# Row chains of a four-layer graph network laid further apart, and eight row scalings moved from GpSimd to ScalarE

## What is computed

```
layer 0: XW = mobius_matvec(W, x); gamma = 2 / max(1 - |XW|^2, eps)
         two_mean = (adj @ (gamma * XW)) / clamp(adj @ (gamma - 1))
         result = expmap0(relu(logmap0(mobius_scalar_mul(rowsum(adj), mobius_scalar_mul(0.5, two_mean)))))
layer 1: a_hat = adj + I; d = rowsum(a_hat)^-0.5; result = (d * a_hat * d @ x) @ W.T + b
layer 2: dis = clip(rowsum(adj), 1)^-0.5; sim = cosine similarities of all rows of x (4096 x 4096)
         attn = softmax(beta * sim * adj, axis=1)
         result = (dis * adj * dis) @ x - x + sigmoid(alpha) * (attn @ x - x)
layer 3: msg = relu((adj @ x) @ W_msg.T + b_msg); result = gru_cell(msg, x, W_ih, W_hh, b_ih, b_hh)
```

## Time and profile before

| | us |
|---|---|
| median of 3 runs | 1555.27 |
| lowest and highest | 1553.88, 1557.45 |
| profiled execution, its own time | 1554.37 |
| its span, first to last instruction | 1552.6 |
| PE busy | 1340.4 (86%) |
| PE weight loads busy | 1026.7 (66%) |
| DVE busy | 1063.1 (68%) |
| ACT busy | 1068.0 (69%) |
| POOL busy | 627.2 (40%) |
| DMA | 413 MB, mean 266 GB/s |

### The profile page before, as it was taken

The page is one execution under the profiler, slowest core; times in us unless marked ns, Lnnn a source line. Parts: engine busy times, 40 slices in busy tenths (PEclk is TensorE's granted clock), DMA queues, the critical chain, the costliest instruction groups (busy, mean ns, idle before and its releaser), DMA issues. The chain is left out here.

```text
span 1552.6 us, 21041 instructions
## 1 busy us (share of the span) xinstructions
PE 1340.4 (86%) x7640; PEld 1026.7 (66%) x7640; DVE 1063.1 (68%) x1928; ACT 1068.0 (69%) x1368; POOL 627.2 (40%) x457
## 2 busy tenths in 40 slices
PE   4599998999887989896499999999998889998885
PEld 4599898898774777772265656656666666665553
DVE  5245555555656989986477887887877986766664
ACT  4578877788675766754386877878778566565563
POOL 4302212222344342336976776767666720000000
PEclk8699999999998999998799999999999999998998
DMA  9399999999955978881386867878776868666640
GB/s 311 124 364 347 342 349 333 341 343 358 314 206 198 336 255 320 304 348 70 147 309 221 321 247 272 275 248 303 256 279 207 296 251 364 213 237 228 224 169 14
DMA packets 114808, 413.08 MB, mean 266 GB/s; under 512 B 10000, under 2 KB 23568, under 8 KB 90128
## 3 DMA queue, kind: packets, MB, share of 16 engines
q1 hardware_dynamic: 106256, 407.54, 73.2%
q10 hardware_dynamic: 8448, 4.20, 0.9%
HBM read 340.40 MB, written 71.30 MB: 265 GB/s over the span
## 5 line engine op out<-in xcount | busy, mean ns | idle before, releaser
L1330 DVE TENSOR_TENSOR part_l<-arena,part_h 128x1024 fp32r<-128x1024 f32 x256 | 326.4, 1301 | 109.3 <-ACT part_h L795 107.8
L795 ACT ACTIVATE part_h<-arena 128x1024 fp32r<-128x1024 f32 x256 | 267.3, 1056 | 167.1 <-PE acc L529 159.9
L1047 POOL TENSOR_TENSOR part_l<-arena,part_h 128x512 fp32r<-128x512 f32 x237 | 304.0, 1297 | 142.6 <-ACT part_h L829 142.6
L1209 DVE TENSOR_TENSOR part_l<-arena,part_h 128x1024 fp32r<-128x1024 f32 x128 | 162.2, 1273 | 179.2 <-ACT part_h L747 178.7
L829 ACT ACTIVATE part_h<-arena 128x512 fp32r<-128x512 f32 x256 | 158.2, 623 | 131.5 <-DVE arena L1404 130.9
L520 PE MATMUL acc<-part_h,Y 128*128 128x512 f32 x512 | 226.9, 443 | 5.9 <-ACT part_h L795 5.9
L521 PE MATMUL acc<-part_h,Y 128*128 128x512 f32 x512 | 208.2, 407 | 0.0
L1010 POOL TENSOR_TENSOR sc<-sc,power 128x4 f32<-128x4 f32 x32 | 51.5, 1611 | 383.5 <-DVE sc L1235 383.4
L584 PE MATMUL strip_b<-ident,arena 128*128 128x128 f32 x1024 | 158.1, 278 | 32.9 <-POOL arena L1043 18.5
L584 PEld LDWEIGHTS strip_b<-ident,arena 128*128 128x128 f32 x1024 | 128.4, 143 | 87.0 <-DVE arena L1404 23.2
L529 PE MATMUL acc<-part_l,Y 128*128 128x512 f32 x512 | 166.2, 406 | 12.0 <-DVE part_l L1330 11.7
(11 more groups left out here) (258 smaller groups left out, 2831.2 us busy)
## 6 DMA issues: line engine op xcount, KB each, us to landing
arena<-adj_t SPq DMA_DIRECT2D x128, 1024.0 KB, 5.1
arena<-in_adj SPq DMA_DIRECT2D x64, 1024.0 KB, 8.5
adj_t<-arena SPq DMA_DIRECT2D x64, 1024.0 KB, 8.9
arena<-in_adj SPq DMA_DIRECT2D x128, 512.0 KB, 6.0
part_h<-adj_t SPq DMA_DIRECT2D x64, 512.0 KB, 5.0
part_l<-adj_t SPq DMA_DIRECT2D x64, 512.0 KB, 5.0
scratch<-v ACTq DMA_DIRECT2D x8, 256.0 KB, 10.1
arena<-scratch SPq DMA_DIRECT2D x8, 256.0 KB, 5.5
```

What stands on the lines that cost most here:

```text
L795: act.activation(flat(part_h[:, slot:slot + 2, :]), turned_pair(n), ACT.Copy).then_inc(high_done, 1)
L1047: pool.tensor_tensor(part_l[:, b % 4, :], mixed[b % G_SLOTS], part_h[:, b % 4, :].bitcast(F32), ALU.subtract).then_inc(low_done, 1)
L1209: dve.tensor_tensor(flat(part_l[:, slot:slot + 2, :]), full_pair(n), flat(part_h[:, slot:slot + 2, :]).bitcast(F32), ALU.subtract).then_in ...
L1330: dve.tensor_tensor(flat(part_l[:, slot:slot + 2, :]), turned_pair(n), flat(part_h[:, slot:slot + 2, :]).bitcast(F32), ALU.subtract).then_ ...
```

## The change

Four things change; no step of the computation is added or left out.

- Hops are laid further apart. `HOOKS` becomes 15 in layer 1 (from 13) and 26 in layer 3 (from 21), and `rows2` uses 20 instead of 12. The starts of chains move with them: layer 1 has 30, 40, 48, 64, ... (before 30, 38, 48, 64, ...), layer 3 has 30, 43, 56, 69, 82, 96, 112, 128 (before 30, 38, 52, 64, 80, 96, 112, 128).

| step (engine) | hop before | hop after |
|---|---|---|
| layer 1: turn_unit (PE), unit_high (ACT), unit_low (DVE) | 10, 11, 12 | 12, 13, 14 |
| layer 2: x_scale (POOL), turn_back (PE), combine (DVE) | 0, 2, 4 | 2, 8, 10 |
| layer 2: statistics (DVE), power (POOL), ln_out (DVE), store (ACT queue) | 5, 6, 8, 12 | 12, 14, 17, 20 |
| layer 3: message (PE), message_act (ACT) | 2, 3 | 3, 4 |
| layer 3: gate_r, gate_z, hidden_n (PE) | 4, 5, 6 | 6, 7, 8 |
| layer 3: r_act (ACT); z_act and hidden_bias (ACT) | 7; 7 | 8; 10 |
| layer 3: input_n (PE), r_times and n_in (DVE), n_act (ACT) | 8, 9, 10 | 12, 13, 14 |
| layer 3: h_minus_n, z_times with h_new (DVE), turn_new (PE) | 11, 12, 14 | 16, 17, 19 |
| layer 3: combine, statistics (DVE), power (POOL), ln_bias (DVE) | 15, 16, 17, 18 | 20, 21, 22, 23 |
| layer 3: ln_out (ACT), store (ACT queue) | 19, 20 | 24, 25 |

- Layer 0's last chain takes one hop a turn in layer 1: hop n + 3 at turn n on VectorE and GpSimd, hop n + 1 on ScalarE. `y_scale` and `y_low` of group 7 move from turn 16 to 24, `y_high` from 18 to 26.
- `scale` of layer 2's rows 0 to 3 is done by ScalarE, as for all others, in steps 4 and 5 of the eight that follow the row; the semaphore `scaled_first` goes, and the waits count on `scaled` alone.
- Layer 2's last chain takes three hops a turn in layer 3's first 8 turns, instead of two. VectorE gets a short loop after layer 1's last turn for the hops that now reach past it.

```diff
-ROWS_FROM = {l: [TURNS.index((0, PAIRS - 1)) + 1, TURNS.index((1, PAIRS - 1)) + 7, PAIRS * 3 + (4 if l == 3 else 0)]
-             + [PAIRS * (s + 1) for s in range(3, SLABS)] for l in (1, 3)}
+ROWS_FROM = {1: [TURNS.index((0, PAIRS - 1)) + 1, TURNS.index((1, PAIRS - 1)) + 9] + [PAIRS * (s + 1) for s in range(2, SLABS)],
+             3: [TURNS.index((0, PAIRS - 1)) + 1, 43, 56, 69, 82] + [PAIRS * (s + 1) for s in range(5, SLABS)]}
...
-HOOKS = {1: 13, 3: 21}
+HOOKS = {1: 15, 3: 26}
...
             def turn2(b):
...
-                    pe.wait_ge(*scaled_at(4 * s + 3, j // 16))
+                    pe.wait_ge(scaled, 8 * s + 7 + j // 16)
...
             for n in range(TURNS_ALL):
                 if n < PAIRS // 2:
-                    rows2(2 * n, SLABS - 1)
-                    rows2(2 * n + 1, SLABS - 1)
+                    for k in range(3 * n, 3 * n + 3):
+                        rows2(k, SLABS - 1)
...
         def _(act):
                 if k == 8:
                     act.wait_ge(row[par], row_before(3, s, "r_act"))
                     act.activation(spare(own + 2), rows_b, ACT.Tanh, scale=0.5, bias=half_bias[:, 0:1]).then_inc(row[par], 1)
+                if k == 10:
                     act.wait_ge(row[par], row_before(3, s, "z_act"))
...
                 high(1, n)
                 if n == 4:
                     y_high(1, SLABS - 2)
-                if n < PAIRS:
-                    rows0(2 * n, SLABS - 1)
-                    rows0(2 * n + 1, SLABS - 1)
-                if n == PAIRS + 2:
+                if 2 <= n < 26:
+                    rows0(n + 1, SLABS - 1)
+                if n == 26:
                     y_high(1, SLABS - 1)
...
-                    if at in (4, 5) and r >= Q:
+                    if at in (4, 5):
                         scale(r, at - 4)
...
         def _(pool):
-            def scale(r, h):
-                pool.wait_ge(weights, r + 1)
-                mine = unit_halves(r, h)
-                pool.tensor_scalar(mine, mine, weight[:, r % 2:r % 2 + 1], None, ALU.mult).then_inc(scaled_first, 1)
...
                                        ALU.add).then_inc(row[par], 1)
+                if k == 2:
                     before("x_scale")
...
             for n in range(TURNS_ALL + HOOKS[1]):
-                if n < PAIRS:
-                    rows0(2 * n, SLABS - 1)
-                    rows0(2 * n + 1, SLABS - 1)
+                if n < 24:
+                    rows0(n + 3, SLABS - 1)
                 if n == 4:
                     y_low(1, SLABS - 2)
-                if n == PAIRS:
+                if n == 24:
                     y_scale(1, SLABS - 1)
                     y_low(1, SLABS - 1)
...
-                if n // 8 - 1 in range(Q) and n % 8 in (4, 5):
-                    scale(n // 8 - 1, n % 8 - 4)
...
         def _(dve):
-                    dve.wait_ge(*scaled_at(r - 2, 1))
+                    dve.wait_ge(scaled, 2 * r - 2)
...
                 low(1, n)
-                if n < PAIRS:
-                    rows0(2 * n, SLABS - 1)
-                    rows0(2 * n + 1, SLABS - 1)
+                if n < 24:
+                    rows0(n + 3, SLABS - 1)
                 for k, s in hooks(1, n - DVE_LEAD):
+                    rows1(k, s)
+            for n in range(TURNS_ALL - DVE_LEAD, TURNS_ALL):
+                for k, s in hooks(1, n):
                     rows1(k, s)
```

More of the change, by code:

```diff
@@ L280, in low_at @@
             return low_done, product_base[l] + n - skipped + 1
-        def unit_halves(r, h):
-            a, b = sorted((unit_of(4 * r + 2 * h), unit_of(4 * r + 2 * h + 1)))
-            return unit_in[:, a:b + 1:b - a, :]
-        def scaled_at(r, h):
-            return (scaled_first, 2 * r + h + 1) if r < Q else (scaled, 2 * (r - Q) + h + 1)
         def unit_loads(k):
@@ L541, in rows1 @@
                     last.then_inc(row[s % 2], 1)
-                if k == 10:
+                if k == 12:
                     pe.wait_ge(row[s % 2], row_before(1, s, "turn_unit"))
@@ L603, in rows2 @@
             def rows2(k, s):
-                if k == 2:
+                if k == 8:
                     pe.wait_ge(row[s % 2], row_before(2, s, "turn_back"))
@@ L624, in rows3 @@
                     last.then_inc(row[par], 1)
-                if k == 2:
+                if k == 3:
                     pe.wait_ge(row[par], row_before(3, s, "message"))
@@ L664, in _ @@
                 if n == 6:
-                    rows1(10, SLABS - 1)
+                    rows1(12, SLABS - 1)
                 if n < NB * SLABS:
@@ L809, in rows1, with halves @@
                     normed(1, s, lambda q: x_nat[:, Q * s + q, :])
-                if k == 11:
+                if k == 13:
                     act.wait_ge(row[s % 2], row_before(1, s, "unit_high"))
                     act.activation(unit_h[:, SLAB * s:SLAB * (s + 1)], rows_b, ACT.Copy).then_inc(row[s % 2], 1)
+            def halves(r, h):
+                a, b = sorted((unit_of(4 * r + 2 * h), unit_of(4 * r + 2 * h + 1)))
+                return unit_in[:, a:b + 1:b - a, :]
             def exponentials(r, h):
                 act.wait_ge(peaks, r + 1)
-                mine = unit_halves(r, h)
+                mine = halves(r, h)
                 act.activation(mine, mine, ACT.Exp, bias=neg_peak[:, r % 2:r % 2 + 1],
@@ L833, in rows2 @@
                     read_acc(2, s)
-                if k == 12:
+                if k == 20:
                     act.wait_ge(row[s % 2], row_done(2, s, "ln_out"))
@@ L863, in rows3 @@
                     normed(3, s, lambda q: v_of[par][:, q, :])
-                if k == 20:
+                if k == 25:
                     act.wait_ge(row[par], row_done(3, s, "ln_out"))
@@ L1359, in rows1 @@
                                       ALU.max).then_inc(row[par], 1)
-                if k == 12:
+                if k == 14:
                     before("unit_low")
@@ L1417, in before @@
                     dve.wait_ge(row[par], row_before(2, s, name))
-                if k == 4:
+                if k == 10:
                     before("combine")
@@ L1423, in rows2 @@
                     last.then_inc(row[par], 1)
-                if k in (5, 8):
-                    layer_norm(2, (5, 8).index(k), s, lambda q: v[:, q, :])
+                if k in (12, 17):
+                    layer_norm(2, (12, 17).index(k), s, lambda q: v[:, q, :])
             def rows3(k, s):
@@ L1434, in before @@
                     dve.wait_ge(row[par], row_before(3, s, name))
-                if k == 9:
+                if k == 13:
                     before("r_times")
@@ L1450, in rows3 @@
                                              ALU.add).then_inc(row[par], 1)
-                if k == 15:
+                if k == 20:
                     before("combine")
@@ L1455, in rows3 @@
                                       ALU.add).then_inc(row[par], 1)
-                if k == 16:
+                if k == 21:
                     layer_norm(3, 0, s, None)
-                if k == 18:
+                if k == 23:
                     before("ln_bias")
@@ L1486, in _ @@
                 if n == 6:
-                    rows1(12, SLABS - 1)
+                    rows1(14, SLABS - 1)
                 if n < NB * SLABS and n % 2 == 1:
```

28 lines of the change are left out of this document (13 added, 15 removed).

## The result

| | before | after |
|---|---|---|
| median (runs beside each other) | 1554.96 us (4) | 1468.28 us (4) |
| lowest and highest | 1553.88, 1557.45 | 1464.88, 1473.03 |
| ratio, 95% interval | | 0.9443 [0.9412, 0.9473] |
| profiled execution, its span | 1554.4, 1552.6 | 1469.7, 1467.9 |
| mean granted clock | 0.950 | 0.964 |

In a second comparison the changed kernel had 1470.86 and the ratio 0.9451 [0.9425, 0.9477]. One of its five executions there, the profiled one, took 1876.98 us at a granted clock of 0.65; the ratio leaves it out, and its profile isn't used. The forecast of 1472 and its range 1457 to 1492 held. The table compares the two spans stage by stage. The marks are the starts of VectorE's low parts (`low(l, n)`) and turn2(0); layer 2's slabs are counted further down from VectorE's first mix of each. Rounding moves a length or a gain by up to 0.1.

What follows compares the result with a forecast made beforehand. PE was taken as the fullest engine nearly everywhere, but stalled by waits on other engines and partly at 1.2 GHz. Terms summed to 83.2 us off 1554.4, giving 1471.2; the median, 0.9 above, was forecast at 1472, range 1457 to 1492.

Steps and rivals of the forecast that it cites:

- Part 1: Layer 2's first rows scaled by ScalarE: turn2(0) starts earlier, 12.5 us gained (10 to 14), ScalarE the new limit.
- Rival (d): Something other than the scaled halves holds turn2(0), so the ScalarE scaling gives 0: 1484 us, chance 0.04.
- Part 2: Layer 0's last chain at one hop a turn in layer 1: 11 us gained (5 to 15), y_scale priced at 2.6.
- Part 3: Layer 1's later hops: 1.7 us over five slabs, VectorE being late next, plus 2 from the first two chains.
- rival (b): More comes: PE at full clock everywhere, layer 1's slabs gain their whole 1.85 us: 103 gained, 1452 us, chance 0.12.
- Part 4: Layer 2's later hops: 23 us over six slabs (15 to 29), slab 7 1.5, layer 3's start net 0.
- Part 5: Layer 3's hops with two turns between: most of 26.9 us of PE waits and clock losses go, 35 gained (24 to 41).
- 6 left over: Layer 3: of the 26.9 us of listed PE waits, 6 us were expected to remain after the change.
- 11 + 3: Layer 3: 11 us back from time at 1.2 GHz, plus 3 us from waits too small to be listed.
- Part 6: Kernel's end: slab 6's longer chain runs behind the last low, PE idles about 3 us, 3.5 lost (2 to 5).
- (a): Rival: in-order queues hand waits on, half of layers 2 and 3 and 5.5 us more come back: 1507 us, chance 0.17.
- (c): Rival: slower, overlapping layer 3 chains let ln_out block high copies, 7 us a chain: 1640 us, chance 0.03.

Runs made afterwards that it cites:

- unit_turn10: Changed kernel with TensorE's turn_unit back at hop 10, unit_high and unit_low staying at 13 and 14: ratio 0.9513 to the kernel before, span 1477.9 us.
- part1_alone: Kernel before, with only ScalarE scaling the halves of layer 2's rows 0 to 3: ratio 0.9926 to the kernel before, span 1538.5 us.
- part2_alone: Kernel before, with only layer 0's last chain at one hop a turn in layer 1: ratio 0.9930 to the kernel before, span 1539.0 us.
- slab2_start50: Changed kernel with the chain of layer 1's slab 2 from turn 50 instead of 48: ratio 0.9428 to the kernel before, span 1465.1 us.
- halves_shared: Changed kernel with second halves of layer 2's rows 0, 1 and 2 scaled by GpSimd again: ratio 0.9407 to the kernel before, span 1465.1 us.

## Why the prediction was right, and where its terms failed

**Part 1 (12.5; 13.3 alone).** The way of pricing held: not the 27.7 us that the instructions save, but the cycle of the new limiting engine. The cycle was 8.65, not 8.9; turn2(0) started with row 3's first half as said. Rival (d) is out.

**Part 2 (11; 9.5 alone).** Turns 0 to 23 went from 53.9 to 40.8, close to VectorE's bound of 38.75. The price of y_scale, turns 24 to 27, was 3.0, not 2.6, and turns 28 to 47 lost 0.6 that I had not listed.

**Part 3 (3.7; 7.4 alone).** Wrong twice. The step "removing PE's wait leaves 0.36: VectorE is late next" read one low that ended 0.36 us before TensorE asked for it. That low had waited for a high copy, which had waited for the product that TensorE's wait held back. unit_turn10 shows it: a slab gains 1.55 of the 1.85. That was in rival (b), at 0.12, and the sign "slabs still about 26.8 us" fell with it (25.6). And of "the first two chains lose a wait for x_bias too" (2 us) more than that came, 2.9 us in turns 28 to 47; but the next chain got a wait that I had put at nothing, which took the 3.0 back in turns 48 to 63: TensorE and GpSimd meet there as the hops of two chains fall together. I had not listed the turns at which slab 1's later hops and slab 2's first ones come on GpSimd.

**Part 4 (23 + 1.5 + 0; 18.7, -1.5 and -2.4 in the changed kernel).** For slabs 1 to 6 I had 3.8 a slab and they gave 3.1: what stays is mainly one wait of turn2 of 1.21 a slab for VectorE, where ln_bias (1.22) and ln_out (2.03, beside two low parts of GpSimd) stand ahead of a mix. Slab 7 was to gain 1.5 and lost 1.5 (49.9 to 51.3 us from its first mix to layer 3's first low; the missing 1 us of the 18.2 lies ahead of slab 1). Slab 7 has waits of the shortened steps for GpSimd's and VectorE's low parts, and hangs on the last pair's transfer; that transfer I hadn't looked at. Layer 3's start was put at net 0, with "the last chain gives back about 1". Three hops a turn put VectorE's hop 12 and GpSimd's 14 into the same turn and VectorE's 17 into the next; two a turn had put 5, 6 and 8 into three turns in a row.

**Part 5 (35; 40.5 for turns 28 to 127, 38.7 with the end).** The mechanism held: one turn more between hops, and no engine takes its place. The slabs took 30.9 to 33.0, "about 32", and the named waits shrank from 26.9 to 2.5, under my 6 left over. The term was too small by these 3.5 and by the clock with the small waits, for which I had 11 + 3. The two windows split the 40.5: TensorE's idle time fell from 26.9 to 3.0 us, and its busy time from 205.4 to 188.8, 16.6 us, with the clock from 0.94 to 1.00 (752 and 744 matmuls are in the records). By the rule of the Trainium skill that the prediction weighed ("TensorE: Matmul & The Clock Gate", section "Terms": half of the throttled time is lost) the term was 37.5, nearer to what came than mine.

**Part 6 (-3.5; nothing that can be told from scatter).** The end in the changed kernel:

```profile
1441.38 0.60 PE L614 MATMUL strip_b<-ident,arena 128*128 128x128 f32 x4
1442.44 0.66 PE L637 MATMUL mid<-ident,arena 128*128 128x128 f32 x4 [0.46 <-DVE arena L1437]
...
1458.67 0.69 PE L637 MATMUL strip_a<-ident,arena 128*128 128x128 f32 x2 [4.44 <-DVE arena L1437]
```

turn_new of slab 6 does come behind the last product, but it waits 0.46 us, not about 3. From slab 7's turn_h to its turn_new it takes 17.29 us, before 16.56 (1526.78 to 1543.34). That is no effect of the change either: with the hops of before it took 17.5 in part1_alone and 18.2 in part2_alone, with the later hops 16.35 in slab2_start50 and halves_shared. (Between the 40.5 and the 38.7 lie this 0.7 and 1.1 us by which slab 7's turn_h now comes later behind the last low part.) I had laid all six steps from r_times on behind the last low, where all but the last lie beside TensorE's last turns.

**Rivals.** (a) did not come: layer 3's TensorE is busy 188.8 of 191.8 us. (c) did not come: no high copy of layer 3's turns 28 to 127 waits for ln_out. (b) was right on layer 1's slabs. Too little for part 1 (0.8), part 3 (3.7) and parts 5 and 6 (38.7 - 31.5 = 7.2), 11.7 us together, stood against too much for part 2 (1.5), layer 2 (24.5 - 18.2 = 6.3), layer 3's start (2.4) and the first stretch (1.4), 11.6 together; the 1.4 left over no run assigns. So the median was hit by luck as well as by working; either side alone would have given 1460 or 1484, still in the range.

## What to carry to other kernels

Before you say that an engine "is late next", follow its own last wait back: if that leads to the stall that you remove, the engine need not be the bound, even at a busy share of 91%. When chains of steps are laid into a loop by hand, write down for each engine at which turns the hops of neighbouring chains fall together; a later hop is free only if it doesn't land on the next chain's first one. And a long wait of one engine may cost next to nothing (ScalarE's 7.23 us), so take it away in an experiment before you count it.
